# A cross-attention and mixture-of-experts kernel: scratch, one affine pass and slot assignment rearranged

## What is computed

```
x = x + block1(layernorm(x), ctx)        # block1 is:
    y = layernorm(z + attention(z, z)) * g1 + b1      # 16 heads of 64
    y = layernorm(y + attention(y, ctx)) * g2 + b2
    h = gelu(y @ fc1_w + fc1_b)                        # 256 -> 1024
    y = layernorm(y + h @ fc2_w + fc2_b) * g3 + b3
x = x + block2(layernorm(x))             # block2 is, n = layernorm(x):
    shared = (gelu(n @ w1s) * (n @ w2s)) @ w3s
    e = argmax(n @ Wg)                   # one expert of 8 for each row
    routed = (gelu(n @ W1[e]) * (n @ W2[e])) @ W3[e]
```

## Time and profile before

| what | value |
|---|---|
| median of 3 runs | 1245.56 us (1244.93 to 1246.37) |
| the profiled execution | 1244.36 us, of which the span of instructions is 1242.6 us |
| TensorE busy, mean granted clock | 1218.9 us (98%), 0.997 |
| VectorE busy | 995.5 us (80%) |
| ScalarE busy | 875.4 us (70%) |
| GpSimd busy | 705.0 us (57%) |
| chain that ended last | TensorE 78%, VectorE 7%, ScalarE 5%, issue 4%, GpSimd 4%, DMA 1% |

### The profile page before, as it was taken

One profiled execution on the slowest core, in us unless ns is written; L12 is line 12 of the kernel. 1 busy time (PEld: TensorE's weight loads), 2 busy tenths in 40 slices (PEclk: granted clock), 3 DMA queues, 4 the chain that ended last, 5 costly groups with the idle time before them and its releaser, 6 DMA issues.

```text
span 1242.6 us, 31390 instructions
## 1 busy us (share of the span) xinstructions
PE 1218.9 (98%) x10415; PEld 1165.9 (94%) x10415; DVE 995.5 (80%) x2685; ACT 875.4 (70%) x2261; POOL 705.0 (57%) x1100
## 2 busy tenths in 40 slices
PE   8899999999999999999999999899999999999998
PEld 6899999999999999999999999899999999999898
DVE  6898988988989988888888888754454888888964
ACT  5788887888888888878878877544333776777642
POOL 4676656656678856555555578876515222334451
PEclk9999999999999999999999999999999999999999
DMA  6060000000000003200000010010004677877722
GB/s 195 2 244 22 2 18 19 2 18 19 2 27 27 2 27 121 77 27 27 2 27 27 2 36 27 27 49 30 1 20 152 224 267 270 267 247 249 264 82 92
DMA packets 74383, 100.60 MB, mean 81 GB/s; under 512 B 5616, under 2 KB 53616, under 8 KB 74224
## 3 DMA queue, kind: packets, MB, share of 16 engines
q1 hardware_dynamic: 72688, 94.40, 23.1%
q0 software_dynamic: 1536, 4.20, 1.1%
HBM read 84.16 MB, written 14.42 MB: 79 GB/s over the span
## 4 chain that ended last, share of the span: by engine, by line
PE 78%; DVE 7%; ACT 5%; issue 4%; POOL 4%; DMA 1%; POOLq 0%; DVEq 0%; ACTq 0%
PE ps_pj L52 9%; PE ps_pj L54 9%; PE ps_pj L53 9%; PE ps_t L949 8%; PE ps_s L939 8%; PE ps_pv L962 8%; PE ps_aux L52 3%; PE ps_aux L54 3%; PE ps_aux L53 3%; ACT probs L1268 3%; PE ps_s L52 3%; PE ps_s L54 3%; PE ps_s L53 3%; PE ps_pv L54 2%; PE ps_pv L53 2%
## 5 line engine op out<-in xcount | busy, mean ns | idle before, releaser
L666 POOL TENSOR_SCALAR probs<-probs,inv 128x256 f32<-128x256 f32 x512 | 237.2, 483 | 224.1 <-DVE inv L1512 223.4
L1268 ACT ACTIVATE probs<-scores,nb 128x256 f32<-128x256 f32 x512 | 253.6, 497 | 18.4 <-DVE nb L1502 17.9
L1502 DVE CUSTOM_DVE_ANT_0 scores<-ps_s,maskf 128x256 f32<-128x256 f32 x512 | 186.8, 421 | 51.3 <-PE ps_s L939 49.2
L1275 ACT ACTIVATE probs_t_hi<-ps_t 128x512 fp32r<-128x512 f32 x256 | 150.8, 590 | 103.4 <-PE ps_t L949 103.4
L1516 DVE TENSOR_TENSOR probs_t_lo<-ps_t,probs_t_hi 128x512 fp32r<-128x512 f32 x256 | 173.1, 676 | 0.2
L949 PE MATMUL ps_t<-ident,probs 128*128 128x128 f32 x1024 | 139.9, 279 | 0.6 <-POOL probs L666 0.6
L962 PE MATMUL ps_pv<-probs_t_lo,v_stack 128*128 128x256 f32 x512 | 130.6, 287 | 0.8 <-issue 0.7
L962 PE MATMUL ps_pv<-probs_t_hi,v_stack 128*128 128x256 f32 x512 | 127.8, 282 | 0.0
L949 PEld LDWEIGHTS ps_t<-ident,probs 128*128 128x128 f32 x1024 | 109.7, 141 | 17.8 <-POOL probs L666 0.9
L52 PE MATMUL ps_pj<-xq_hi,wq_lo 128*128 128x256 f32 x368 | 115.3, 313 | 3.3 <-POOL wk_lo L713 3.2
L685 POOL TENSOR_TENSOR heads_t_lo<-joined,heads_t_hi 128x256 fp32r<-128x256 f32 x128 | 95.1, 743 | 33.4 <-ACT heads_t_hi L1284 33.0
(11 more groups left out here) (285 smaller groups left out, 4480.6 us busy)
## 6 DMA issues: line engine op xcount, KB each, us to landing
raw<-in_L_ffn_W SPq DMA_DIRECT2D x96, 512.0 KB, 4.7
slot_rows<-hin SPq DMA_DIRECT2D x3, 768.0 KB, 5.9
rows<-in_x SPq DMA_DIRECT2D x8, 256.0 KB, 2.7
after_self<-rows SPq DMA_DIRECT2D x8, 256.0 KB, 2.1
rows<-after_self SPq DMA_DIRECT2D x8, 256.0 KB, 2.8
cin<-in_ctx SPq DMA_DIRECT2D x8, 256.0 KB, 3.0
after_cross<-rows SPq DMA_DIRECT2D x8, 256.0 KB, 2.2
stage<-in_L_xattn_fc_w SPq DMA_DIRECT2D x2, 1024.0 KB, 9.3
```

The lines of the kernel that those rows point to most:

```text
L666: last = pool.tensor_scalar(PR[:, h, t, :], PR[:, h, t, :], inv[:, h, t:t + 1], 1.0, ALU.mult, ALU.mult)
L1268: last = act.activation(PR[:, h, t, :], SM[:, h, t, :], ACT.Exp, bias=nb[:, h, t:t + 1], scale=-1.0, accum_out=sums[:, h, t:t + 1])
L1275: act.activation(flat(PT[0][:, i % 2, h, :, :]), ps_t[h][:, :], ACT.Copy).then_inc(t_hi, 1)
L1502: last = dve.tensor_tensor_reduce(SM[:, h, t, :], ps_s[h][:, t * S:(t + 1) * S], maskf[:, i // PAIRS % 2, :], -SCALE, -LOWEST, ALU.add, AL ...
```

## The change

It does six things. The statistics tiles get a third row, which the dense steps use (VectorE's `row_stats` and GpSimd's `norm_rows` alike), and the wait of the first `dense_stats` for `y_ready` is gone. `affine_output` of the last attention rows is done by GpSimd after `norm_second(2)`, and the store of these rows stands in SyncE's queue ahead of the last `load_h`. TensorE makes the transposes of step 1 ahead of the last `attend`. VectorE makes `shared_lows` ahead of the first low part of step 1, no longer behind it. In step 8, ScalarE and VectorE take the split of the transposed normed rows behind chunk 1, no longer ahead of the split of chunk 0. `assign_slots` stands at the end of step 9, no longer behind the first gate of step 10. No instruction is added or removed but for waits.

```diff
--- before.py
+++ after.py
@@ -313,8 +313,8 @@
         warm = at("warm", 140 * KB, [P, 512], BF16)
         mhalf = little("mhalf", [P, ST])
         nb, sums, inv = (little(n, [P, 2, ST]) for n in ("nb", "sums", "inv"))
-        part, mv = little("part", [P, 2, ST, 6]), little("mv", [P, 2, ST, 2])
-        veps, rstd, nmean = (little(n, [P, 2, ST]) for n in ("veps", "rstd", "nmean"))
+        part, mv = little("part", [P, 3, ST, 6]), little("mv", [P, 3, ST, 2])
+        veps, rstd, nmean = (little(n, [P, 3, ST]) for n in ("veps", "rstd", "nmean"))
         b1 = little("b1", [P, FC])
         WG, wg_raw = little("wg", [P, KC, 2, E], F32R), little("wg_raw", [P, KC, E])
         position, slot_expert = little("position", [P, TT], I32), little("slot_expert", [P, SLOTS], I32)
@@ -601,8 +601,9 @@
                             .then_inc(landed, 16)
             load_x(0)
             load_x(1)
-            store(NTURN - 1)
             for n in range(3, DENSE):
+                if n == DENSE - 1:
+                    store(NTURN - 1)
                 load_h(n)
                 load_x(n - 1)
             load_x(DENSE - 1)
@@ -730,7 +731,7 @@
 
                 h = hin[:, n % 3, :, :]
                 pool.wait_ge(fstat_ready, n + 1)
-                link(norm_rows(1, h, h))
+                link(norm_rows(2, h, h))
                 link(pool.tensor_tensor(h, h, both(g3_b[:, :]), ALU.mult))
                 pool.wait_ge(xb_ready, n + 1)
                 pool.tensor_tensor(x2[:, 2 * n:2 * n + 2, :], h, xin[:, n % 2, :, :], ALU.add).then_inc(x2_ready, 1)
@@ -847,7 +848,6 @@
                 split_late(i)
             bias_rows(0)
             norm_output(NTURN - 1)
-            affine_output(NTURN - 1)
             for n in range(DENSE):
                 if n + 1 == DENSE:
                     routing_constants()
@@ -857,6 +857,8 @@
                 if n == 1:
                     pool.wait_ge(shared_lo, len(SHARED_PIECES))
                 norm_second(n)
+                if n == 2:
+                    affine_output(NTURN - 1)
             count_tiles()
             place()
             scatter()
@@ -1185,11 +1187,12 @@
                 extra = extra_event(i)
                 if extra is not None and extra[0] != "h":
                     {"v": project_v, "xq": transpose_rows, "xc": transpose_ctx}[extra[0]](extra[1])
+                if i == NPAIR:
+                    transpose_step(1)
                 if 1 <= i <= NPAIR:
                     attend(i - 1)
                 if NPAIR <= i < NPAIR + 2:
                     up_dense(0, i - NPAIR + 2)
-            transpose_step(1)
             down(0, range(FC))
             for step in range(1, STEPS):
                 after_single = is_single(step - 1)
@@ -1413,13 +1416,13 @@
                     weight_hi(load, (10, 11))
                     continue
                 gelu_glu(step, 0)
-                if step == DENSE:
-                    hi_of_x(("l", step - 2))
                 if splits:
                     weight_hi(load, (0, 1))
                 for j in range(1, HP):
                     hi_glu(step, j - 1)
                     gelu_glu(step, j)
+                    if step == DENSE and j == 1:
+                        hi_of_x(("l", step - 2))
                     if splits:
                         weight_hi(load, (2 * j, 2 * j + 1))
                 hi_glu(step, HP - 1)
@@ -1613,11 +1616,8 @@
 
             def dense_stats(n):
                 dve.wait_ge(y_done, n + 1)
-                if n == 0:
-                    dve.wait_ge(y_ready, NTURN)
-                else:
-                    dve.wait_ge(x2_ready, n)
-                row_stats(1, hin[:, n % 3, :, :], fstat_ready)
+                wait(dve, x2_ready, n)
+                row_stats(2, hin[:, n % 3, :, :], fstat_ready)
 
             def second_stats(n):
                 dve.wait_ge(x2_ready, n + 1)
@@ -1742,10 +1742,10 @@
                         dense_stats(step - 1)
                     if step >= 2:
                         lo_of_x(("l", step - 2))
+                    if step == 1:
+                        shared_lows()
                     if step >= 1:
                         lo_of_hidden(step, 0)
-                    if step == 1:
-                        shared_lows()
                     for j in range(1, HP):
                         lo_of_hidden(step, j)
                         if step == 0 and j == 1:
@@ -1784,17 +1784,15 @@
                     weight_lo(load, 10)
                     continue
                 gate(step, 0)
-                if step == DENSE:
-                    lo_of_x(("l", step - 2))
                 if step == DENSE + 1:
                     choose()
-                if step == DENSE + 2:
-                    assign_slots()
                 if splits:
                     weight_lows(load, (0, 1))
                 for j in range(1, HP):
                     lo_of_hidden(step, j - 1)
                     gate(step, j)
+                    if step == DENSE and j == 1:
+                        lo_of_x(("l", step - 2))
                     if j == 1 and is_single(step - 1):
                         finish(step - 1)
                     if splits:
@@ -1808,6 +1806,8 @@
                     weight_lows(load, range(8, WPIECES))
                 if step == DENSE:
                     lo_of_x(("l", DENSE - 1))
+                if step == DENSE + 1:
+                    assign_slots()
                 if step == DENSE + FRONT + SLOTS:
                     for t in range(FRONT, B):
                         add_found(t)
```

## The result

| | kernel before | changed kernel |
|---|---|---|
| first comparison, median of 4 runs each | 1245.82 us (1244.93 to 1246.37) | 1237.24 us (1236.48 to 1237.45) |
| ratio, 95% interval | | 0.9931 (0.9914 to 0.9948) |
| second comparison, 17 and 6 runs | 1245.53 us | 1238.31 us (1237.06 to 1239.27) |
| ratio, 95% interval | | 0.9943 (0.993 to 0.9955) |
| profiled execution, its span | 1244.36, 1242.6 us | 1237.3, 1235.6 us |

The change is faster, by 7.2 to 8.6 us where 6.0 were forecast.

What follows compares the result with a forecast made beforehand. TensorE, busy 98% of the span, was taken as the bound, so only its waits could be won: 3.6 + 0.8 + 1.55 = 6.0 us off, a median of 1239.6 us, range 1238.2 to 1242.0.

Steps and rivals of the forecast that it cites:

- rival 3: Routed steps, paced by VectorE or weights, take the lead back behind 930 us: 1242 to 1245.6 us; chance 0.10.
- First normed batch, 3.6 us: Transposes of the first normed dense batch come 3.6 us earlier, as GpSimd's chain ends at 800.4, not 803.98.
- GpSimd's chain runs for 13.0 us from 787.4: GpSimd's work from first dense norm to `norm_second(0)` starts at 787.4, keeps its 13.0 us and ends at 800.4.
- TensorE's own bound of 4.1 us: At the first normed batch, TensorE by itself could be 4.1 us earlier; the upper bound if GpSimd's chain gets shorter.
- Rival 1: GpSimd stands for all 2.4 us of `shared_lows`: 3.6 becomes 2.1, sum 4.5, time 1241.1 us; chance 0.16.
- Step 8, 0.8 us: TensorE's wait of 0.59 us in step 8 for a low part goes, worth 0.8 us.
- `assign_slots`, 1.55 us: Step 10's low part no longer comes 1.31 us late behind slot assignment; 1.55 us won, with 1.5 us of slack.
- Rival 4: VectorE's scan wait at the end of step 9 delays step 10: 1248 us and above; chance 0.02.
- Affine pass later, nothing: Two passes, 2.7 us, behind `norm_second(2)` fit in GpSimd's 3.0 us of waiting per dense step; booked at nothing.
- Rival 2: The later affine pass makes `normed(3)` late by up to 2.7 us: sum 3.3, time 1242.3 us; chance 0.06.
- uncovered it would cost at most its 2.4 us: In step 1, the moved `shared_lows` cost nothing under cover; without it, TensorE loses at most their 2.4 us.
- 0.36, 1.5 and 2.27 us: TensorE's savings up to the first normed batch: step 1's transposes moved, `down(1)` wait gone, wait for GpSimd gone.

Runs made afterwards that it cites:

- e13: Changed kernel with VectorE's four shared weight passes (`shared_lows`) left out: 1238.29 us, ratio 0.9942 to the kernel before.
- e4: Changed kernel with `assign_slots` put back in step 10, behind its first gate: 1239.49 us, ratio 0.9949 to the kernel before.
- e5: Changed kernel run once more with no edit, beside the kernel before: 1238.31 us, ratio 0.9943.
- e10: Changed kernel with two more affine passes on GpSimd behind the third second norm: 1237.61 us, ratio 0.9936 to the kernel before.
- e2: Changed kernel with the affine pass put back ahead of the first dense norm: 1241.06 us, ratio 0.9964 to the kernel before.

## Why the prediction was right or wrong

- **What bounds it: right.** All that was won is idle time of TensorE, and nothing was taken back later (rival 3 is out: the lead only grows).
- **First normed batch, 3.6 us: too small.** The step that failed is "GpSimd's chain runs for 13.0 us from 787.4". I carried the 13.0 over as though VectorE would hit the same passes of GpSimd in the new order. It measured 12.16 us: `shared_lows` hit shorter passes (0.93 us in place of 1.28), and the bias pass over `xin` now starts ahead of VectorE's low parts of `w3s` and no longer behind them (0.49 us). Then TensorE's own bound of 4.1 us decided, which stood in the text as the upper end; measured 4.34, and no wait for GpSimd was left where I had kept 0.5 us. Rival 1 is out: GpSimd lost 0.93 us to `shared_lows` (`e13`), not their whole 2.4. That VectorE's passes delay GpSimd is real.
- **Step 8, 0.8 us, and `assign_slots`, 1.55 us: right.** 0.83 and 1.57 us; `e4` gives 1.5 for the second, taken alone (1.0 against `e5`). Rival 4 is out: VectorE had the scan at 913.40, the 918.3 of the prediction less the 4.9 us that all of step 9 was earlier, so it used none of the 1.5 us of slack.
- **Affine pass later, nothing: right** in both ways (`e10`, and 3.4 us lost in `e2`). Rival 2 is out.
- **`shared_lows` "uncovered it would cost at most its 2.4 us": wrong.** Its price depends on what GpSimd does at the time: 0.6 us a pass beside short passes, 1.7 beside long two-input ones, plus about 2 us for the 4.0 us that TensorE then runs at half clock. The forecast did not rest on it, since the cover was there.
- **The sum.** 0.36, 1.5 and 2.27 us held within 0.25 us together, 0.8 and 1.55 nearly to the hundredth: 6.7 in place of 6.0. The remaining 0.6 us are a wait in the last step of that one execution of the kernel before. The rows on which the prediction rests end at 957 us, so it could not hold this wait.
- **The range.** It gave 0.9 us to the spread of the runs. The last attention wait comes at 755.50 to 758.25 us in the 19 profiled executions, whatever the kernel, so two medians of four runs can be off by more. Of the 2.6 us by which the first difference of medians (8.6) exceeds the sum (6.0), 0.7 are the change's, 0.6 the wait in the last step and 1.3 this spread. That the first median fell outside the range and the second inside it is thus mostly chance. The 5.4 us at the lower end of the sum's own range have no working.

## What to carry to other kernels

A wait for a buffer that two stages share can hide a second one behind it, on the other engine: free the buffer, and also move what the other engine does ahead of it. Here the scratch alone kept 1.0 of 6.7 us, and the changed kernel without the second move lost 3.4. Before placing VectorE passes with two SBUF inputs, look at what GpSimd does at that time: beside its small passes they cost their own length, beside its long two-input passes nearly three times that. And price a wait of TensorE by what stands behind it too: read the granted clock of the next 6 us. A wait of 2.76 us cost twice its idle in one execution here; a wait of 2.94 us in another had no fall behind it.

## What the runs showed of the hardware

- The granted clock behind waits in the middle of steady work: 1.00 behind 1.24, 2.00, 2.06 and 2.08 us; 0.67, 0.58, 0.50 and 0.50 in the 3.7 to 4 us behind 2.32, 2.68, 2.76 and 4.74 us. Each is one execution. Behind the wait of 2.32 us the clock was 1.00 for another 1.2 us and then 0.51 for 3.5; behind that of 2.76 it was 0.50 for 6.0 us.
- Early in the kernel, where TensorE has more waits, length tells less: behind the wait of 2.86 to 2.96 us near 46.5 us the clock stayed at 1.00 in four executions and was 0.50 to 0.70 in fifteen. Behind a wait of only 1.07 to 1.08 us near 25.8 us it was 0.54 to 0.62 in five executions and 1.00 in fourteen.
- The start of the kernel, which is the same in all 19 profiled executions and has waits of some us: in the four whose granted clock over the first 50 us is 1.00, the last attention wait comes at 755.50 to 755.86; in the fifteen with 0.93 to 0.98, at 756.59 to 758.25. Part of the spread between executions is thus the clock at the start; what decides it, and the 1.7 us among the fifteen, are open.
- VectorE and GpSimd on SBUF together: the table above. The weight passes of the routed slots show it too: `wk_lo` takes 1653 ns on the mean of 16 and `wq_lo` 726 ns on the mean of 34 in the changed kernel, for the same operation and size.
